# A recurrence with routed experts: another order for the last three groups and the first tiles

## The reference

```
xn = layernorm(x)                                  # x: 4 x 2048 x 512
h[t] = h[t-1] * A + xn[t];   s = h @ BC            # A: 512, BC: 512 x 512
chosen = argmax(xn @ gate_w.T)                     # 8 experts
g = silu(xn + xn @ expert_w[chosen].T)
out = x + s * g
```

## Time and profile before

| | |
|---|---|
| median of 3 runs | 516.22 us (515.95 to 517.01) |
| the profiled execution | 516.83 us |
| its span, first to last instruction | 515.1 us |
| TensorE matmul busy | 495.1 us (96%) |
| VectorE busy | 410.1 us (80%) |
| GpSimd busy | 322.4 us (63%) |
| ScalarE busy | 260.1 us (50%) |
| mean granted TensorE clock | 0.991 |

### The profile page before, as it was taken

How to read it: one execution, slowest core, us unless ns; L and a number is a source line. 1 busy time by engine, 2 the same in 40 slices (tenths; PEclk the granted TensorE clock), 3 DMA queues, 4 the chain that set the end, 5 groups by cost and what they waited for, 6 DMA issues and landing times. The chain is left out here.

```text
span 515.1 us, 10723 instructions
## 1 busy us (share of the span) xinstructions
PE 495.1 (96%) x2739; PEld 388.5 (75%) x2740; DVE 410.1 (80%) x1075; ACT 260.1 (50%) x500; POOL 322.4 (63%) x362
## 2 busy tenths in 40 slices
PE   7999999999999999999988999999999999999993
PEld 6667777777777777777766888888788888887882
DVE  5999899989899989898844777777777777776773
ACT  4676776786687677677422333333333333333330
POOL 2567666666766766766663766656666666646652
PEclk9999999999999999999998999999999999999997
DMA  7978788887877877876245577777777776766620
GB/s 235 350 264 263 222 258 248 246 243 234 271 226 244 271 208 259 257 228 213 104 113 203 185 244 241 237 234 243 234 229 231 230 239 215 231 208 206 216 83 9
DMA packets 65538, 114.27 MB, mean 222 GB/s; under 512 B 9994, under 2 KB 28042, under 8 KB 65504
## 3 DMA queue, kind: packets, MB, share of 16 engines
q1 hardware_dynamic: 47328, 62.46, 39.1%
q0 software_dynamic: 18176, 51.47, 31.7%
HBM read 65.96 MB, written 55.08 MB: 235 GB/s over the span
## 5 line engine op out<-in xcount | busy, mean ns | idle before, releaser
L1073 PE MATMUL ps_s<-w_hi,split 128*128 x284 | 118.3, 417 | 0.1
L643 ACT ACTIVATE ps_s<-ps_s 128x512 f32<-128x512 f32 x71 | 41.3, 582 | 151.5 <-PE ps_s L1075 151.5
L509 POOL DMA_INDIRECT out_dram<-work x71 | 73.2, 1032 | 68.9 <-DVE work L890 59.0
L1074 PE MATMUL ps_s<-w_lo,split 128*128 x284 | 112.6, 396 | 0.0
L1075 PE MATMUL ps_s<-w_hi,split 128*128 x284 | 112.4, 396 | 0.0
L418 POOL TENSOR_TENSOR split<-work,split 128x1024 fp32r<-128x1024 f32 x32 | 77.5, 2421 | 48.6 <-ACT split L571 48.5
L977 PE MATMUL ps_s<-bc_hi,split 128*128 128x512 f32 x256 | 104.1, 407 | 0.7 <-DVE bc_lo L790 0.6
L978 PE MATMUL ps_s<-bc_lo,split 128*128 128x512 f32 x256 | 101.3, 396 | 0.0
L499 POOL DMA_INDIRECT work<-token_rows,work x67 | 69.6, 1038 | 21.7 <-issue 19.8
L436 POOL DMA_INDIRECT slot_table<-token_id,slot_id x64 | 63.0, 984 | 31.6 <-issue 21.1
L685 DVE TENSOR_TENSOR_SCAN work<-a_col,work,ps_xt 128x256 f32<-128x256 f32 x112 | 74.2, 721 | 0.0
(11 more groups left out here) (118 smaller groups left out, 737.9 us busy)
## 6 DMA issues: line engine op xcount, KB each, us to landing
token_rows<-work SPq DMA_DIRECT2D x31, 528.0 KB, 3.2
work<-in_L_attn_inputs_dram SPq DMA_DIRECT2D x31, 512.0 KB, 4.7
token_rows<-work SPq DMA_DIRECT2D x29, 512.0 KB, 5.5
work<-in_L_ffn_expert_w_dram SPq DMA_DIRECT2D x128, 64.0 KB, 4.2
slot_table<-w_lo SPq DMA_DIRECT2D x1, 2080.0 KB, 12.8
token_rows<-in_L_attn_inputs_dram SPq DMA_DIRECT2D x3, 512.0 KB, 10.6
out_dram<-work POOLq DMA_INDIRECT x71, 3.3
work<-token_rows,work POOLq DMA_INDIRECT x67, 4.4
```

Source lines behind the costliest of these rows:

```text
L509: nc.gpsimd.indirect_dma_start(out=out_flat, out_offset=bass.IndirectOffsetOnAxis(ap=slot_tok[:, n:n + 1], axis=0), in_=o_sb[:, u], in_off ...
L1073: nc.tensor.matmul(z_ps[v], hi, wh, start=(k == 0), stop=False)
L1074: nc.tensor.matmul(z_ps[v], hi, wl, start=False, stop=False)
```

## The change

It concerns the last three groups (29, 30 and 31; `TAIL = 29`) and the first tiles.

- TensorE: the turns, scores and ranks of groups 30 and 31 are placed ahead of most s products of groups 29, 30 and 31. `product_hi` can now be made in parts.
- VectorE: the low part of the last group moves from GpSimd to VectorE, behind the plan; the weight blocks 29, 30 and 31 follow it there. The ranks of group 30 are placed between the scans of group 31.
- ScalarE: both halves of group 31 are normalised ahead of the head copy of group 30; s of groups 28 to 31 is copied later, the last group's behind weight block 31.
- GpSimd: ids of group 31 are scattered without a low part before; ids of three tiles and all lines are fetched ahead of the wait for the s stores, and then all gathers follow. `FIRST` is 3, so gather 3 takes its tokens from `slot_tok`. The place of the lines in SBUF stays where it was.
- TensorE between the stages: 26 filling matmuls and no wait among them, instead of 35. In the tiles 0, 1 and 2 the next tile's turn lies within the expert matmuls.

```diff
-    FIRST = 4
+    FIRST = 3
+    TAIL = GROUPS - 3
...
@@ GpSimd
-            for c in range(GROUPS - 2):
-                group(0, c, left=GROUPS - 1 - c)
-            count(0, GROUPS - 2)
-            scatter_ids(0, GROUPS - 2)
-            low_part(0, GROUPS - 1)
-            next_ids(0, GROUPS - 1)
-            scatter_ids(0, GROUPS - 1)
-            add_identity(0, GROUPS - 1)
+            for c in range(TAIL):
+                group(0, c)
+            count(0, TAIL)
+            scatter_ids(0, TAIL)
+            low_part(0, TAIL + 1)
+            count(0, TAIL + 1)
+            next_ids(0, TAIL + 1)
+            scatter_ids(0, TAIL + 1)
+            next_ids(0, TAIL + 2)
+            scatter_ids(0, TAIL + 2)
+            add_identity(0, TAIL + 1)
+            add_identity(0, TAIL + 2)
...
             first_ids(0)
             first_ids(1)
+            first_ids(2)
+            pool.wait_ge(lo_done, GROUPS)
+            all_ids()
             for v in range(2):
                 pool.wait_ge(s_stored[v], 16 * (GROUPS // 2 + (TPG - 1 if v == LAST else 0)))
-            gather(0, 0)
-            first_ids(2)
-            all_ids()
-            gather(0, 1)
-            gather(0, 2)
-            first_ids(3)
+            for c in range(3):
+                gather(0, c)
             for c in range(3, RR):
                 gather(0, c)
...
@@ ScalarE, behind the groups up to TAIL - 1
+            block_high(0, TAIL - 1)
+            copy_tail(0, TAIL + 1)
+            for t in range(TPG):
+                normalise(0, TAIL + 2, t)
+            copy_head(0, TAIL + 1)
+            copy_parts(0, TAIL + 1)
+            copy_tail(0, TAIL + 2)
+            block_high(0, TAIL)
+            high_part(0, TAIL + 1)
+            take_s(0, TAIL - 1)
+            copy_head(0, TAIL + 2)
+            copy_parts(0, TAIL + 2)
+            take_s(0, TAIL)
+            high_part(0, TAIL + 2)
+            take_mv(0, TAIL + 1)
+            take_mv(0, TAIL + 2)
+            for t in range(TPG):
+                take_half(0, TAIL + 1, t)
+            block_high(0, TAIL + 1)
+            block_high(0, TAIL + 2)
+            for t in range(TPG):
+                take_half(0, TAIL + 2, t)
...
@@ VectorE
+            scan(0, TAIL + 1)
+            block_low(0, TAIL - 1)
+            turn_w(TAIL)
+            route(0, TAIL + 1, False)
+            scan(0, TAIL + 2, between=True)
+            route(0, TAIL + 2, False, behind=False)
+            place(0, TAIL + 2, 0)
+            nc.vector.tensor_scalar(tile_i[:, 0], count_ps, float(P - 1), None, ALU.add).then_inc(plan_step, 1)
+            place(0, TAIL + 2, 1)
...
-            block_low(0, GROUPS - 2)
-            turn_w(GROUPS - 1)
-            block_low(0, GROUPS - 1)
+            dve.wait_ge(hi_done, GROUPS)
+            dve.wait_ge(lo_done, GROUPS - 1)
+            nc.vector.tensor_tensor(hs_lo[LAST], hs[:, LAST], hs_hi[LAST], ALU.subtract).then_inc(lo_done, 1)
+            for c in range(TAIL, GROUPS):
+                block_low(0, c)
+                if c + 1 < GROUPS:
+                    turn_w(c + 1)
...
@@ TensorE
+            group(0, TAIL - 1)
+            a, b, c = TAIL, TAIL + 1, TAIL + 2
+            turn_x(0, b)
+            product_hi(0, a, 0)
+            ranks(0, a)
+            product_lo(0, a, 0)
+            score_parts(0, b)
+            turn_x(0, c)
+            scores(0, b)
+            product_hi(0, a, 1)
+            ranks(0, b)
+            product_lo(0, a, 1)
+            product_hi(0, b, 0, part=range(1))
+            score_parts(0, c, placed=True)
+            product_hi(0, b, 0, part=range(1, 2))
+            scores(0, c)
+            product_hi(0, b, 0, part=range(2, CH))
+            product_hi(0, b, 1, part=range(1))
+            ranks(0, c, counted=True)
+            product_hi(0, b, 1, part=range(1, CH))
+            product_lo(0, b, 0)
+            product_lo(0, b, 1)
+            product_hi(0, c, 0)
+            product_hi(0, c, 1)
+            product_lo(0, c, 0)
+            product_lo(0, c, 1)
...
-            stay_busy(18)
-            pe.wait_ge(ids2_loaded[0], 16)
-            stay_busy(17)
+            stay_busy(26)
...
+                    if isinstance(it, int) and it + c < FIRST and k == CH - 3:
+                        turn_x2(0, c + 1)
                     if isinstance(it, int) and it + c == 0 and k == CH - 2:
                         turn_slots()
...
-            tile(0, 0, ahead=False)
-            turn_x2(0, 1)
-            for c in range(1, RR):
-                tile(0, c)
+            for c in range(RR):
+                tile(0, c, ahead=c >= FIRST)
```

More of the change, by code:

```diff
@@ L575, in block_high, with take_mv @@
                 nc.scalar.copy(block_of(w_hi, it, c), w_turned).then_inc(w_hi_done, 1)
-            def take_s(it, c):
+            def take_mv(it, c):
                 v = c % 2
@@ L603, in _, with group @@
             root(0, 2)
-            def group(it, c, left=3, start=False):
+            def group(it, c, start=False):
                 if not start:
                     block_high(0, c - 1)
-                if left >= 1:
-                    copy_tail(it, c + 1)
-                    copy_head(it, c + 1)
+                copy_tail(it, c + 1)
+                copy_head(it, c + 1)
                 if not start:
@@ L614, in group @@
                     copy_parts(0, 1)
[L615 to L619, removed]
-                    copy_parts(it, c + 1)
[L621 to L630, removed]
+                high_part(it, c + 1)
+                normalise(it, c + 2, 0)
+                if not start:
+                    copy_parts(it, c + 1)
+                normalise(it, c + 2, 1)
+                root(it, c + 3)
+            for c in range(TAIL):
+                group(0, c, start=(c == 0))
+            block_high(0, TAIL - 1)
[20 more added lines that the diff above has]
+                take_half(0, TAIL + 2, t)
             act.wait_ge(root_loaded, 1)
@@ L673, in variance, with scan @@
                 last.then_inc(var_ready, 1)
-            def scan(it, c):
+            def scan(it, c, between=False):
                 n = U * it + c
@@ L682, in scan @@
                     if k == CH // 2:
+                        if between:
+                            place(it, c - 1, 0)
+                            place(it, c - 1, 1)
                         dve.wait_ge(xnt_tail, n + 1)
@@ L734, in route @@
                     place(it, c - 1, 0)
-                points = bank_score if n < 3 or n == GROUPS - 1 else score
+                points = bank_score if n < 3 or n > TAIL else score
+                order = bank_score if n > TAIL else ranked
                 nc.vector.tensor_reduce(points[:, :, :], score_ps.rearrange("p t k e -> p t e k"), AX.X,
@@ L745, in route @@
                 for t in range(TPG):
-                    last = nc.vector.scalar_tensor_tensor(ranked[:, t], points[:, t], top[:, t:t + 1],
+                    last = nc.vector.scalar_tensor_tensor(order[:, t], points[:, t], top[:, t:t + 1],
                                                           prio[:, t], ALU.is_equal, ALU.mult)
@@ L751, in route @@
                 dve.wait_ge(gate_step, 5 * n + 3)
-                nc.vector.tensor_reduce(first[:, :], ranked[:, :, :], AX.X, ALU.max).then_inc(gate_step, 1)
+                nc.vector.tensor_reduce(first[:, :], order[:, :, :], AX.X, ALU.max).then_inc(gate_step, 1)
                 if ahead:
@@ L758, in route @@
                 for t in range(TPG):
-                    last = nc.vector.tensor_scalar(onehot[:, v, t], ranked[:, t], first[:, t:t + 1], None,
+                    last = nc.vector.tensor_scalar(onehot[:, v, t], order[:, t], first[:, t:t + 1], None,
                                                    ALU.is_equal)
@@ L798, in _, with group @@
             route(0, 0, False, behind=False)
[L800 to L810, removed]
+            def group(it, c, start=False):
+                scan(it, c + 1)
+                if not start:
                     block_low(0, c - 1)
@@ L814, in group @@
                         deviation(0, 2, step)
[L815 to L828, removed]
+                statistics(it, c + 3)
+                dve.wait_ge(stats_done, U * it + c + 4)
+                wait(dve, mv_taken, U * it + c)
+                dve.sem_inc(mv_free, 1)
+                variance(it, c + 3)
+                turn_w(c)
+                route(it, c + 1, True)
+            for c in range(TAIL):
+                group(0, c, start=(c == 0))
+            dve.wait_ge(table_empty, 16)
+            scan(0, TAIL + 1)
[7 more added lines that the diff above has]
+            place(0, TAIL + 2, 1)
             def step(ins, k):
@@ L966, in ranks, with product_hi @@
                 last.then_inc(rank_done, 1)
-            def product_hi(it, c, t, first=False):
+            def product_hi(it, c, t, first=False, part=range(CH)):
                 v = c % 2
@@ L972, in product_hi @@
```

(2 more changed lines are left out.)

44 lines of the change are left out of this document (16 added, 28 removed).

## The result

The changed kernel takes 521.83 us (median of 4 runs, 521.50 to 522.96) against 516.48 us for the kernel before (4 runs): a ratio of 1.0097, 95% interval 1.0068 to 1.0126. It is 5.35 us slower; forecast were +1.1 us and a range that ended at 519.3. The profiled execution took 522.96 us with a span of 521.0.

The account below looks back on a forecast made before the run. The prediction took TensorE as the bound, with the change acting only at the junction of the stages. Tile 3's later start gave +1.0, the clock made it +1.1 on the 516.22 us median: 517.3 us, range 515.0 to 519.3.

Parts of the forecast that it names:

- So the products still end at 259.1: TensorE, end of the first stage: three short waits replace the 0.73 us one-hot wait, so the end stays at 259.1.
- at 250.4: VectorE, start of placing: 0.42 us after the ranks of group 31 start, as before.
- 4.9 us: VectorE's time from placing to the end of the plan, almost unshortened by three first tiles instead of four.
- 1.2: VectorE's new subtraction for group 31, in us, with bounds 0.69 and 2.39.
- end at about 262.8: GpSimd: three fetches of ids and the block of lines finish then, covered by the wait for the s store.
- +0.5 us: Gather 0: the later store of the last s rows, not the ids, now sets its start, 264.8 against 264.29.
- I add 0.1 for it: Tile 0: cost in us of TensorE's clock fall after a 4.7 us wait, bounds 0 and 0.6.
- the row lands 4.2 us later: Row 3: lands at 281.5, 4.2 us after its gather starts at 277.3.
- Rival two: No change: list of slots or gather takes about 1 us less, row 3 isn't late, 516.2 us; chance 0.21.
- +1.0, with the clock +1.1 us: Summed loss up to tile 3's start, 286.25 against 285.27 before, plus 0.1 for the clock at tile 0.
- rival one: Before tile 2: the 2.3 us wait for row 3 halves TensorE's clock, +1.7, so 519.0 us; chance 0.24.
- the sum itself: Whole kernel: the added-up terms hold, likeliest 517.3 us, covering 516.6 to 518.0; chance 0.36.

Follow-up runs that it names:

- experiment 2: Changed kernel with FIRST 4 again and a fourth fetch of ids ahead of the block of lines, so row 3 uses its own ids; 519.10 us, ratio 1.0003.
- experiment 1: Changed kernel with both halves of s of group 31 copied ahead of weight block 31; 521.09 us, ratio 1.0054.
- experiment 5: New order of the last three groups alone, with the head of stage 2 as in the kernel before; 518.02 us, ratio 1.0031.
- Experiment 4: Changed kernel with 46 filling matmuls between the stages instead of 26; 520.77 us, ratio 1.0033.
- experiment 3: Changed kernel with 12 filling matmuls added ahead of tile 2; 521.13 us, ratio 1.0050.
- experiment 6: New head of stage 2 alone, with the last groups as in the kernel before; 522.29 us, ratio 1.0110.
- experiment 7: Changed kernel with s of group 31 copied before weight block 31, FIRST 4, block of lines and fourth ids behind three gathers; 515.46 us, ratio 0.9966.
- experiment 8: As experiment 7, but with 37 fillers instead of 26; 515.60 us, ratio 0.9984.
- experiment 10: As experiment 7, but block of lines and fourth ids right behind gather 0, and 37 fillers; 513.75 us, ratio 0.9956.
- experiment 9: As experiment 7, but block of lines and fourth ids right behind gather 0, with 26 fillers; 515.46 us, ratio 0.9984.

## Why the prediction was wrong

The sign and the places were right: an s store made late by weight block 31, gather 3 behind the list of slots, TensorE waiting before tile 2. The size wasn't. Counted from the products' end (259.1 in the forecast, 260.13 measured):

| step | forecast | measured |
|---|---|---|
| ranks of group 31 | -9.2 | -9.2 |
| last s copy ends | +2.7 | +3.2 |
| gather 0 | +5.7 | +6.4 |
| tile 0's experts | +13.9 | +15.0 |
| gather 3 | +18.2 | +19.5 |
| row 3 normalised | +22.4 | +24.7 |
| tile 2's experts | +23.5 | +26.0 |
| tile 3's experts (turn of tile 4 and 0.35) | +27.1 | +31.3 |

- **"So the products still end at 259.1", "at 250.4", "4.9 us", "1.2":** right. The products end at 260.13 in this trace, but in the ten traces with the new tail they end between 258.30 and 260.13, and in the three with the old one between 259.12 and 259.50: no cost of the new tail shows. VectorE's new subtraction took 1.21 us, without the 0.5 us of contention that I had weighed. What missed on the way to the last store is that block 30's turn waited 0.78 us for GpSimd, behind the scatters of 1.55 and 1.79 us. That these two were slow by contention is not shown: experiment 2 ran the same order with scatters of 1.00 and 0.97 us.
- **"end at about 262.8"** (the fetches of ids and the block of lines, +3.7): too early. The block's issue ended at 265.23, +5.1. In the changed kernel the later store hid this; in experiment 1 it set gather 0.
- **"+0.5 us" for the last store:** the mechanism is shown by experiments 1 and 5; it measured +1.2 (gather 0 at 6.4 instead of 5.2 us).
- **"I add 0.1 for it"** (the clock at tile 0): mis-sized. The wait was 5.46 us, half clock lasted until 276.5 instead of 273.5, and from the normalise of row 0 to the experts went 4.13 us instead of 3.85, and to the list of slots another 0.2 more. Experiment 4 measured what not letting it fall at all gives up to tile 2's start: 2.1 us.
- **"the row lands 4.2 us later":** row 3 took 5.2 us (279.63 to 284.85), in experiments 1, 3 and 4 5.0 to 5.1. It took 4.3 in experiment 6 (old tail, ids from the list) and in experiments 5, 7 and 8 (new tail, own ids). So the longer time shows only where the new tail and the list come together; why stays open. Rival two's 1 us less came in no trace.
- **The step that failed** is the stretch from tile 0 to tile 3 in the sum ("+1.0, with the clock +1.1 us"), in two terms. First, it carries nothing for the clock behind the wait before tile 2. I worked out a wait of 2.3 us there and had in hand that one of 1.97 had been followed by half clock, and still put that only in rival one, with 0.24 against 0.36 for the sum itself. The wait was 3.15 us, the clock fell, and that cost 1.6 us (experiment 3; the rival said 1.7). Second, row 3, forecast normalised at +22.4, came at +24.7, and tile 2 started at +26.0 instead of +23.5. The clock alone would have made the sum about 518.9, inside the range; it took the late row as well to leave it. The misses all had one sign: 0.7 to gather 0, 0.4 to tile 0, 0.2 to gather 3, 1.0 for row 3, 0.2 to tile 2, and 1.6 for the clock make up 4.1, the difference between +1.0 and +5.1.

None of the three things happened that I had named as making the prediction wrong: gather 0 didn't start before 263.5, row 3 didn't land before 280.5, and TensorE's waits in the last groups stayed below 0.9 us. Two of them asked about the cheaper side and one about the last groups; none asked whether tile 2 might start later than forecast. The range ended at 519.3, 0.3 above rival one's 519.0, and so had no room for the clock and a late row together.

## What to carry to other kernels

Work taken off a path is worth only as much as the next arrival allows: here the last ranks came 5.1 us sooner, the first fetch of ids 1.7 us sooner and the first gather 1.2 us later (all counted from the products' end), because a copy that was ready stood in ScalarE's queue behind a chain of three engines. When requests are regrouped, ask of each what index or flag it needs, who makes it, and what delays that: with the list as its source, row 3 took over every delay of tile 0, and with its own ids fetched ahead of the gathers (experiment 2) it took none. And in this kernel a wait on TensorE of some 2 us or more had to be priced with the matmuls behind it at half speed. A fill is worth what no later wait takes back: 0.8 us in experiment 4, 0.85 in experiment 8, 1.2 in experiment 10.

## What the runs showed of the hardware

Whether a wait on TensorE is followed by half clock isn't decided by its length alone when it is near 2 us: waits of 1.93 us and 2.08 us (experiment 5) were not, waits of 1.97 us and 2.27 us (experiment 6) were. The half-clock stretch at tile 2 was 3.4 us long in the changed kernel and 6.8 us in experiment 4, at almost the same wait (3.15 and 2.99 us). In the first the clock fell 0.6 us after TensorE had resumed, in the second 0.7 us before, so 6.1 of the 6.8 us lay on matmuls. The Trainium skill, page "TensorE: Matmul & The Clock Gate" (section "What's actually happening"), says that the gate's phase isn't tied to the kernel's start; these rows fit that, since nearly equal waits had unequal consequences.

Three gathers of 532 KB ahead of a small transfer delay it: the block of lines landed 3.8 us after its issue when it went ahead of them (the changed kernel), 4.7 and 4.9 us after it behind one of them (experiments 9 and 10), and 6.3 and 5.4 us after it behind all three (experiments 7 and 8).
